# Linear attention in a one-core graph network: context taken from the normed rows, the last front's norm and softmaxes moved, attention of a joint over five PSUM banks

## The chip, the cores and the metric

One core of one Trainium2 chip runs the whole program in one launch. The metric is the device time in microseconds (us); the median of three runs stands for a kernel. A profile of one execution comes with it.

## The reference

`x` has 3125 rows of 256. After a layernorm the rows go two ways that are added at the end: a relational graph network of two passes over 53,125 edges (gather a row, multiply it with a relation's row, sum by target, three 256x256 products, tanh), and four transformer layers with linear attention:

```
h = layernorm(x) * g1 + b1                      # 3125 x 256, hence k, v: 3125 x 256
q = softmax over each head's 32 channels of (h @ Wq) * scale
k = softmax over the 3125 rows of (h @ Wk) * scale
v = h @ Wv
context = k^T v, per head (8 heads, 32 x 32)
x = x + (q @ context) @ Wo + bo
x = x + gelu(layernorm(x) * g2 + b2 @ W1 ...) @ W2 + b2      # 256 -> 1024 -> 256
```

A last stage (mixture of four experts and a shared network) follows. All is computed in float32.

## The kernel before

**Tiles.** The rows are 25 tiles of 125 (T), in 5 groups of 5 (GT, NG). A layer needs its whole context before any row can go on, so each layer is split: a *front* (norm, q, k, v, both softmaxes, the group's share of the context) runs for a group of rows of layer l+1 while the *feed* part (attention product, norm, up, gelu, down) of layer l works on the next group.

**Stages.** `iteration(lay, gi)` runs the feed of group gi and beside it, from gi = 1 on, the front of group gi-1 of the next layer (class `Front`). The last group's front has nothing beside it but graph work: `joint(la)` runs it (class `Alone`), closes the context, multiplies it by Wo (`cwo`), and does attention, norm and turning for the first group of the layer. For layer 0 all five fronts run as `Alone` before `joint(0)`. So there are 20 fronts: 5 alone in the prologue, 12 beside a feed, 3 alone in the joints of layers 1 to 3. Below, "joint 1" is the one of layer 1.

**A front.** VectorE (DVE) takes statistics (`norm_stats`, L422) and norms tile j into `xha` (L943, L1053; two buffers); TensorE (PE) turns it (L452); ScalarE (ACT) applies gain and shift into `hTa` (L1562, L1638); PE multiplies by Wk and Wv in one product of 512 columns (L1911, L2011) and by Wq in one of 256 (L1915, L2016), each over two chunks of 128 channels, and float32 takes two instructions for each; ACT copies k and v to `kv5` (L1574, L1651), q to `qrow` (L1582, L1658). DVE keeps the running maximum of k (L953), which is turned, reduced, spread again by PE (L1926) and subtracted (L971). ACT takes the exponentials (L1589, L1593), DVE normalizes q (L995 to L1001), PE forms the context, 2 x 5 products of 129 columns (128 of v and a column of ones; L1934), and turns q (`turn_q`), which ACT copies to `qT_all`. `add_context` (L978) adds the group's context, faded by the change of the maximum.

**Closing a joint** (L2073 on): context divided by its sums and masked to the heads on DVE (L1120, L1123), turned on PE (L2083), copied (L1130), times Wo plus bo (L2089, L2091), copied (L1133). `attend` (L1959) for 5 tiles alternates between two banks, so that tile pairs wait for `add_attention` (L1015).

**Graph work** is put between by hand: POOL gathers rows (L753, L760; two gathers per step of 128 edges in the first pass, one in the second) into a ring of 8 steps; DVE builds one-hot keys (L891) and multiplies (L900); PE sums 2 steps a unit into `ps_seg` (L1879), 257 columns each; DVE adds to `acc` (L880). `STEPS_JOINT` and `STEPS_GROUP` say how many steps each stage holds, `marks` and `joint_marks` where; `upto(k)` in each engine's program issues units up to a mark. Each engine works its own list strictly in order.

## Time and profile before

| | us |
|---|---|
| median of 3 runs | 2602.88 (2590.5 to 2606.51) |
| the profiled execution | 2572.66 |
| its span | 2570.9 |
| PE busy | 2110.7 (82%) |
| DVE busy | 1284.4 (50%) |
| ACT busy | 733.5 (29%) |
| POOL busy | 1362.8 (53%) |

"Busy" is the time in which an engine has an instruction in its datapath; the rest is waiting. The granted clock is the share of 2.4 GHz that TensorE was given: its two levels are 1.2 GHz (0.5) and 2.4 GHz (1.0). In a timeline a row merges instructions of one line; "x4" are four instructions, the number behind the start is their length, and the brackets say how long the engine had been idle before and what ended it. The length of the last matmul of a row is modelled, so prices of matmuls are read between starts.

### The profile page before, as it was taken

The numbers are of one execution on the slowest core, as the hardware profiler recorded it, in microseconds if no ns is written. First come the engines' busy times: TensorE is split into PE (matmuls) and PEld (weight loads), VectorE is DVE, ScalarE is ACT, GpSimd is POOL, SyncE is SP. The second block draws the span as 40 slices with busy tenths as digits, with TensorE's granted clock in tenths as the row PEclk, the third lists the DMA queues.
The fourth block names the chain that finished last, engine by engine and source line by source line (L and its number), as shares of the span: only waits on it lengthen the run. The fifth ranks groups of instructions, "written<-read, shape, count | busy, mean of one in ns | idle before, by whom it ended". The sixth has DMA issues, their size and how long they took to land.

```text
span 2570.9 us, 33841 instructions
## 1 busy us (share of the span) xinstructions
PE 2110.7 (82%) x11194; PEld 1738.3 (68%) x11194; DVE 1284.4 (50%) x3362; ACT 733.5 (29%) x1970; POOL 1362.8 (53%) x1377
## 2 busy tenths in 40 slices
PE   3776778987777789878778797998879888889998
PEld 1544667766656577666467686776657777778897
DVE  6765325435453254354523544746665555466533
ACT  3332123323221133232212332322222211223443
POOL 6566666656646666566466125657546665651000
PEclk9897889988888899889788899999989999999999
DMA  7466655545645555456455225545535555550000
GB/s 205 133 181 197 184 164 163 165 145 162 195 141 173 174 155 163 146 155 196 138 177 172 74 70 174 174 145 166 183 123 157 162 168 159 166 98 17 10 20 20
DMA packets 191190, 370.85 MB, mean 144 GB/s; under 512 B 36227, under 2 KB 122548, under 8 KB 191044
## 3 DMA queue, kind: packets, MB, share of 16 engines
q0 software_dynamic: 78272, 225.07, 30.8%
q1 hardware_dynamic: 92856, 128.48, 15.6%
q10 hardware_dynamic: 19916, 15.44, 2.0%
q8 instruction: 81, 1.33, 0.2%
q14 instruction: 65, 0.53, 0.1%
HBM read 304.76 MB, written 64.95 MB: 144 GB/s over the span
## 4 chain that ended last, share of the span: by engine, by line
PE 55%; DVE 14%; another core or an unknown queue 10%; issue 9%; POOL 3%; DMA 3%; ACT 2%; DVEq 1%; ACTq 0%; SPq 0%
PE ps_seg L1879 10%; PE ps_down L1984 8%; PE ps_hid L1975 7%; PE ps_kv L1911 4%; PE ps_x L1959 3%; DVE xg L900 3%; PE ps_down L2207 2%; POOL xg L753 2%; PE ps_kv L2207 2%; PE ps_x L452 2%; PE ps_hid L2227 2%; PE ps_hid L452 2%; DMA xg<-h_rows,idx_tab 2%; PE ps_x L1915 2%
## 5 line engine op out<-in xcount | busy, mean ns | idle before, releaser
L1879 PE MATMUL ps_seg<-xg,hot 128*125 128x257 f32 x1664 | 474.3, 416 | 207.9 <-DVE xg L900 159.7
L753 POOL DMA_INDIRECT xg<-xn_rows,idx_tab x416 | 416.8, 1002 | 419.1 <-PE ps_seg L1879 250.3
L753 POOL DMA_INDIRECT xg<-h_rows,idx_tab x416 | 426.2, 1025 | 284.2 <-PE ps_seg L1879 152.7
L1879 PEld LDWEIGHTS ps_seg<-xg,hot 128*125 128x125 f32 x1664 | 310.9, 202 | 293.4 <-DVE xg L900 152.1
L760 POOL DMA_INDIRECT rg<-relation_rows,idx_tab x416 | 422.4, 1016 | 128.0 <-issue 128.0
L1975 PE MATMUL ps_hid<-hT,wff 128*128 128x125 f32 x3200 | 414.1, 284 | 27.0 <-issue 22.3
L1975 PEld LDWEIGHTS ps_hid<-hT,wff 128*128 128x128 f32 x3200 | 407.6, 201 | 40.7 <-issue 28.2
L1624 ACT ACTIVATE gT<-ps_hid,b1p 128x125 f32<-128x125 f32 x800 | 225.4, 369 | 677.7 <-remote 322.3
L1984 PE MATMUL ps_down<-wff,gT 128*125 128x256 f32 x1600 | 374.8, 386 | 11.1 <-issue 10.7
L900 DVE TENSOR_TENSOR xg<-xg,rg 128x512 f32<-128x512 f32 x416 | 286.0, 687 | 129.8 <-DMA xg<-h_rows,idx_tab 67.7
L1984 PEld LDWEIGHTS ps_down<-wff,gT 128*125 128x125 f32 x1600 | 301.0, 192 | 56.1 <-issue 12.8
L1039 DVE TENSOR_TENSOR xres<-xres,ps_down 125x256 f32<-125x256 f32 x100 | 40.3, 419 | 333.9 <-remote 160.3
L891 DVE TENSOR_TENSOR hot<-iota_t,key_tab 128x250 f32<-128x250 f32 x416 | 170.9, 411 | 7.8 <-issue 5.3
L1015 DVE TENSOR_TENSOR xres<-xres,ps_x 125x256 f32<-125x256 f32 x100 | 38.8, 418 | 184.7 <-PE ps_x L1959 133.1
L1539 ACT ACTIVATE kv<-ps_kv 125x512 f32<-125x512 f32 x74 | 44.2, 597 | 288.4 <-PE ps_kv L1911 198.0
L1959 PE MATMUL ps_x<-cwo,qT_all 128*125 128x256 f32 x400 | 109.3, 417 | 9.4 <-DVE xres L1015 6.9
L880 DVE SCALAR_TENSOR_TENSOR acc<-ps_seg,in_tile,acc 125x257 f32 x208 | 100.4, 483 | 32.7 <-PE ps_seg L1879 14.3
L1911 PE MATMUL ps_kv<-wqkv,hTa 128*125 128x512 f32 x240 | 114.7, 601 | 0.0
L1614 ACT ACTIVATE hT<-ps_x,ln2p 128x250 f32<-128x250 f32 (+1 forms) x120 | 56.6, 523 | 192.2 <-PE ps_x L452 176.8
L1959 PEld LDWEIGHTS ps_x<-cwo,qT_all 128*125 128x125 f32 x400 | 83.1, 211 | 30.1 <-DVE xres L1015 9.7
L424 DVE BATCH_NORM_STATS2 stat<-xres 125x6 f32<-125x256 f32 x200 | 70.1, 413 | 0.0
L1911 PEld LDWEIGHTS ps_kv<-wqkv,hTa 128*125 128x125 f32 x240 | 46.4, 193 | 34.1 <-issue 30.1
(285 smaller groups left out, 2702.0 us busy)
## 6 DMA issues: line engine op xcount, KB each, us to landing
second_relation_rows<-rg SPq DMA_DIRECT2D x104, 512.0 KB
rg<-second_relation_rows SPq DMA_DIRECT2D x104, 512.0 KB
wff<-L_mix_W ACTq DMA_DIRECT2D x8, 1024.0 KB
xg<-xn_rows,idx_tab POOLq DMA_INDIRECT x416
rg<-relation_rows,idx_tab POOLq DMA_INDIRECT x416
xg<-h_rows,idx_tab POOLq DMA_INDIRECT x416
h_rows<-rg SPq DMA_DIRECT2D x25, 112.0 KB
xres<-x POOLq DMA_DIRECT2D x5, 560.0 KB, 8.7
```

Source lines behind the costliest of these rows:

```text
L452: ins = pe.transpose(dst[:, c * T:(c + 1) * T], rows[:, c * P:(c + 1) * P], ident[0:T, 0:T])
L753: pool.indirect_dma_start(xg[:, k, 0:D], None, rows, bass.IndirectOffsetOnAxis(ap=idx_tab[:, step, 0:1], axis=0))\
L760: pool.indirect_dma_start(rg[:, k, :], None, rel_d, bass.IndirectOffsetOnAxis(ap=idx_tab[:, step, 1:2], axis=0))\
L891: dve.tensor_tensor(hot[:, s:s + UNIT, :], iota_t[:, :].unsqueeze(1).broadcast_to([EP, UNIT, T]), key_tab[:, at:at + UNIT].unsqueeze(2).br ...
L900: dve.tensor_tensor(m, m, r, ALU.mult).then_inc(s_msg, 1)
L1624: ins = act.activation(gT[:, j % 2, ff, :], ps_hid[hf][:, f * T:(f + 1) * T], ACT.Gelu, bias=b1p[:, ff:ff + 1])
L1879: ins = pe.matmul(ps_seg[u // UW % 2][0:T, 0:AW], hot[:, s % RING, :], xg[:, s % RING, :], start=s % WIN == 0, stop=s % WIN == WIN - 1)
L1911: ins = pe.matmul(ps_kv[0:T, :], hTa[:, j % 2, c, :], wqkv[:, c, D:], start=c == 0, stop=c == KC - 1)
L1959: ins = pe.matmul(ps_b[j % 2][0:T, :], q[:, c * T:(c + 1) * T], cwo[:, c, :], start=c == 0, stop=c == KC - 1)
L1975: ins = pe.matmul(ps_hid[hf][:, f * T:(f + 1) * T], w1[:, c, ff * P:(ff + 1) * P], hT[:, j, c, :], start=c == 0, stop=c == KC - 1)
L1984: ins = pe.matmul(ps_down[j % 2][0:T, :], gT[:, j % 2, f, :], w2[:, f, :], start=f == 0, stop=f == FC - 1)
L2207: ins = pe.matmul(ps_two[j % 2][0:T, 0:D], gT[:, j % 2, m * KC + c, :], wg[g][:, m, c, :], start=m == 0 and c == 0, stop=m == 2 and c == K ...
```

## The change

1. **No v product.** The context of a head is (k^T xhat) Wv, with xhat the normed row before gain and shift. `xha` and v are gone; the normed rows go to `x5`, which shares a buffer with k (`kx5`, 256 + 257 columns). A tile has one product of 512 columns, for q and k; ACT copies 256 columns of k and 256 of q out of the same bank. The context products have 257 columns in place of 129, into two banks (`ps_beside`: `ps_kv`, `ps_hid[1]`; `ps_alone`), and `add_context` adds 2 x 257 columns.
2. **Closing.** `close_context` divides each half as it comes; four transposes (128 x 128); gain and shift applied on DVE; four products of 128 columns with Wv; mask; Wo into `ps_dn`, with bo multiplied ahead.
3. **The last front's norm** (new class `Last`): statistics of its rows beside the last tiles of the last FFN group, its norm right behind `add_ffn(4)`. The q softmax of the front before it (sum, scale, turn) goes behind that, into the joint.
4. **Softmaxes of the last front in two parts** (tiles 0 to 2, tiles 3 and 4), in joints 0 to 3.
5. **Attention in a joint over five banks** (`ps_att`), with no wait for `add_attention`.
6. Waits: norm(0) of a front waits for the context before it; up(0), second half, waits for `add_context` (layers 0 to 2, gi > 1); the wait for the next layer's q, k, v weights goes from group 0 to group 1; Wv and ln1 are loaded after the Wv product. Numbers of graph steps stay.

```diff
 def norm(self, j):                               # Front, DVE
-    dve.wait_ge(s_tra, self.tn + (j + 1 if j else 2))
-    dve.tensor_scalar(xha[:, j % 2, :], self.row(j), mv[:, j, 0:1], rstd[:, j:j + 1], ALU.subtract, ALU.mult)\
+    if j == 0:
+        dve.wait_ge(s_ctx, self.grp + 1 - self.back)
+    dve.tensor_scalar(self.x5[:, j, 0:D], self.row(j), mv[:, j, 0:1], rstd[:, j:j + 1], ALU.subtract, ALU.mult)\
         .then_inc(s_xha, 1)
...
 def joint(la, upto, one):                        # DVE
     m = joint_marks(la)
-    f = Alone(la, NG - 1) if la else fronts[-1]
+    f = lasts[la]
     if la:
-        f.head(lambda: one(m["head"]))
+        upto(0)
+        before_last[la].q_sum()
+        before_last[la].q_scale()
+        f.k_max(1)
         upto(m["head"])
-        front_tiles(f, None, None, [m[f"tile{j}"] for j in range(GT)], upto, one)
+        f.k_max(2)
+        f.q_max(0)
+        f.q_shift(0)
+        upto(m["tile2"])
+        f.k_max(3)
+        f.q_sum(0)
+        f.q_scale(0)
+        upto(m["tile4"])
     front_end(f, m, upto)
...
 def front_end(f, m, upto):                       # DVE
+    upto(m["spread"])
     f.k_max(GT - 1)
     f.k_top()
-    f.q_max()
-    upto(m["spread"])
-    f.k_shift()
-    f.q_shift()
-    f.q_sum()
-    f.q_scale()
+    f.q_max(1)
+    f.k_shift(0)
+    f.k_shift(1)
+    f.q_shift(1)
+    f.q_sum(1)
+    f.q_scale(1)
     upto(m["ctx"])
-    f.add_context()
+    f.close_context()
...
+def close_context(self):                         # Last, DVE
+    dve.wait_ge(s_kf, self.grp + 1)
+    dve.wait_ge(s_cacc, self.grp + 1)
+    cm = self.cm
+    for c in range(KC):
+        if c == 0:
+            dve.wait_ge(s_c0, self.la + 1)
+        else:
+            dve.wait_ge(s_ctx, self.grp + 2)
+        cm(dve.scalar_tensor_tensor(ctxacc[:, c, :], ctxacc[:, c, :], kfade[:, c:c + 1],
+                                    self.ps_ctx[c][:, 0:AW], ALU.mult, ALU.add))
+        cm.wait()
+        cm(dve.reciprocal(rsum[:, c:c + 1], ctxacc[:, c, D:AW]))
+        cm.wait()
+        cm(dve.tensor_scalar(ctxacc[:, c, 0:D], ctxacc[:, c, 0:D], rsum[:, c:c + 1], None, ALU.mult))
+    cm.wait()
+    dve.sem_inc(s_cacc, 1)
...
 def iteration(lay, gi, upto, one, early):        # DVE
+    a = lasts[lay + 1] if lay < L - 1 and is_last(gi) else None
...
+    if a:
+        for j in range(3):
+            a.stat(j)
...
     b.add_ffn(3)
     b.add_ffn(4)
+    if a:
+        a.stat(3)
+        a.stat(4)
+        norm_rest(dve, a.ln)
+        a.norm(0)
+        a.norm(1)
+        f.add_context()
+        for j in range(2, GT):
+            a.norm(j)
+        before_last[lay + 1] = f
+        return
...
 def qkv(self, j):                                # Front, PE
     pe.wait_ge(s_kve, self.tn + (j + 1))
-    for c in range(KC):
-        ins = pe.matmul(ps_kv[0:T, :], hTa[:, j % 2, c, :], wqkv[:, c, D:], start=c == 0, stop=c == KC - 1)
-    ins.then_inc(s_kv, 1)
     pe.wait_ge(s_qe, self.tn + (j + 1))
     for c in range(KC):
-        ins = pe.matmul(ps_q[0:T, :], hTa[:, j % 2, c, :], wqkv[:, c, 0:D], start=c == 0, stop=c == KC - 1)
+        ins = pe.matmul(ps_kv[0:T, :], hTa[:, j % 2, c, :], wqkv[:, c, 0:2 * D], start=c == 0, stop=c == KC - 1)
     ins.then_inc(s_q, 1)
...
     if la:                                       # joint, PE
-        upto(m["head"])
         f.turn(0)
-        front_tiles(f, None, None, [m[f"tile{j}"] for j in range(GT)], upto)
+        f.turn(1)
+        f.qkv(0)
+        f.turn(2)
+        f.qkv(1)
+        upto(0)
+        f.turn(3)
+        f.qkv(2)
+        for j in range(GT):
+            before.turn_q(j)
+        upto(m["head"])
+        f.turn(4)
+        f.qkv(3)
+        upto(m["tile2"])
+        f.qkv(4)
+        upto(m["tile4"])
     front_end(f, m, upto)
...
+        ins = pe.matmul(ps_kv[:, c * P:(c + 1) * P], wqkv[:, f, 2 * D + c * P:2 * D + (c + 1) * P],
+                        cwo[:, f, c * P:(c + 1) * P], start=f == 0, stop=f == KC - 1)
...
     for j in range(GT):
-        b.attend(j)
+        b.attend_alone(j)
...
 def front_end(f):                                # ACT
-    f.k_exp()
-    f.q_exp()
-    for j in range(0, GT, 2):
-        f.qT_out(j)
+    f.k_fade()
+    f.qT_out(0)
+    f.k_exp(0)
+    f.k_exp(1)
+    f.q_exp(1)
+    f.qT_out(2)
+    f.qT_out(4)
```

In `front_end` on PE the turns of q stand around the context now: turn_q(0), turn_q(1), k_spread, graph unit, turn_q(2), context, turn_q(3), turn_q(4).

## Rows read from the trace of the kernel before

**Rows 1.** The page's busy shares and granted clock in 40 slices

```profile
PE 2110.7 (82%) x11194; PEld 1738.3 (68%) x11194; DVE 1284.4 (50%) x3362; ACT 733.5 (29%) x1970; POOL 1362.8 (53%) x1377
...
PEclk9897889988888899889788899999989999999999
```

**Rows 2.** Busy time by stage: joint 0's fronts, a group, joints 1 and 3

```profile
core 0: us, PE busy (x) PEld busy (x) DVE busy (x) ACT busy (x) POOL busy (x), PEclk, DMA share, GB/s
108.00:202.00 94.00, 77.91 (x328) 52.81 (x328) 63.85 (x148) 36.25 (x77) 64.95 (x64) 0.91 0.57 169
428.00:520.00 92.00, 77.86 (x416) 65.51 (x415) 45.57 (x122) 29.60 (x76) 56.11 (x56) 0.91 0.54 162
686.00:766.00 80.00, 51.96 (x198) 35.70 (x198) 46.33 (x119) 17.39 (x35) 36.56 (x36) 0.77 0.52 158
...
1841.00:1917.00 76.00, 55.23 (x219) 38.46 (x218) 50.64 (x129) 17.50 (x35) 27.97 (x27) 0.82 0.41 128
```

**Rows 3.** PE's timeline at full clock: start, length, instructions

```profile
192.00 1.88 PE L2011 MATMUL ps_kv<-wqkv,hTa 128*125 128x512 f32 x4
193.72 1.03 PE L2016 MATMUL ps_x<-wqkv,hTa 128*125 128x256 f32 x4
194.58 2.40 PE L1934 MATMUL ps_hid<-wff 125*128 125x129 f32 x20
196.81 0.59 PE L452 MATMUL ps_hid<-ident,xh 125*128 125x125 f32 x4
197.24 1.03 PE L1879 MATMUL ps_seg<-xg,hot 128*125 128x257 f32 x4
198.11 1.88 PE L2011 MATMUL ps_down<-wqkv,hTa 128*125 128x512 f32 x4
```

**Rows 4.** What PE waited for in the group from 428 to 520

```profile
PE ps_seg L1879 <- DVE xg L900: 7.8, 1, 7.8
PE ps_x L452 <- DVE qrow L1001: 4.1, 1, 4.1
```

**Rows 5.** PE's timeline, joint 1, and the first product of joint 3

```profile
706.42 3.62 PE L2011 MATMUL ps_kv<-wqkv,hTa 128*125 128x512 f32 x4
...
724.96 0.38 PE L452 MATMUL ps_hid<-ident,kmax 125*128 125x125 f32 x2
...
742.03 0.38 PE L2083 MATMUL ps_kv<-ident,kdiag 128*128 128x128 f32 x2
...
745.78 1.96 PE L1959 MATMUL ps_x<-cwo,qT_all 128*125 128x256 f32 x8
...
1855.79 3.03 PE L2011 MATMUL ps_kv<-wqkv,hTa 128*125 128x512 f32 x4
```

**Rows 6.** DVE's timeline, joint 1, and the last FFN sum before joint 3

```profile
686.45 0.75 DVE L1039 TENSOR_TENSOR xres<-xres,ps_down 125x256 f32<-125x256 f32 x2 [2.08 <-PE ps_down L1984]
687.34 1.49 DVE L995 TENSOR_REDUCE qm<-qrow 125x40 f32<-125x1280 f32 x1
...
689.30 1.49 DVE L1001 TENSOR_TENSOR qrow<-qrow,qm 125x1280 f32<-125x1280 f32 x1
696.79 0.61 DVE L978 SCALAR_TENSOR_TENSOR ctxacc<-ctxacc,kfade,ps_kv 128x129 f32<-128x129 f32 x2 [6.00 <-remote]
...
703.84 0.83 DVE L1055 TENSOR_SCALAR xha<-xres,mv,rstd 125x256 f32<-125x256 f32 x2
...
753.25 0.75 DVE L424 BATCH_NORM_STATS2 stat<-xres 125x6 f32<-125x256 f32 x2
...
1841.01 0.75 DVE L1039 TENSOR_TENSOR xres<-xres,ps_down 125x256 f32<-125x256 f32 x2
```

**Rows 7.** ACT's timeline, joint 1: one tile, and k's exponential

```profile
714.37 0.38 ACT L1539 ACTIVATE qrow<-ps_x 125x256 f32<-125x256 f32 x1 [0.27 <-PE ps_x L2016]
715.46 0.80 ACT L1642 ACTIVATE hTa<-ps_x,ln1p 128x125 f32<-128x125 f32 x2 [0.70 <-PE ps_x L452]
717.18 0.60 ACT L1539 ACTIVATE kv<-ps_kv 125x512 f32<-125x512 f32 x1 [0.91 <-PE ps_kv L2011]
...
731.54 1.27 ACT L1589 ACTIVATE kv<-kv 125x1280 f32<-125x1280 f32 x1 [4.74 <-DVE kv L971]
```

**Rows 8.** POOL's timeline in a group: gathers of the first pass

```profile
455.35 0.94 POOL L753 DMA_INDIRECT xg<-xn_rows,idx_tab  x1 [0.30 <-issue]
456.60 0.95 POOL L760 DMA_INDIRECT rg<-relation_rows,idx_tab  x1 [0.30 <-issue]
457.85 0.95 POOL L753 DMA_INDIRECT xg<-xn_rows,idx_tab  x1 [0.30 <-issue]
```

**Rows 9.** What DVE's idle time ahead of L978 ended on, all 20 contexts

```profile
L978 DVE SCALAR_TENSOR_TENSOR ctxacc<-ctxacc,kfade,ps_kv x24: 341/344/351, 426.3 to 1847.5; 128x129 f32<-128x129 f32 x24
...
  remote: 31.4, 8
```

More of the change, by code:

```diff
@@ L425, in norm_stats, with norm_rest @@
             between()
+            norm_rest(dve, chain, between)
+        def norm_rest(dve, chain, between=lambda: None):
             hold(dve, chain.s, chain.base + chain.n)
@@ L453, in transpose_rows, with parts_done, part_of @@
             return ins
+        PARTS = (slice(0, 3), slice(3, GT))
+        def parts_done(grp, part=0):
+            return grp + grp // NG + (part + 1)
+        def part_of(j):
+            return int(j >= PARTS[1].start)
         def pair(j):
@@ L1361, in z_beside @@
                                               ALU.mult).then_inc(s_exh, 1)
-            fronts = [Alone(0, ga) for ga in range(NG)]
+            lasts, before_last = [Last(la) for la in range(L)], {}
+            fronts = [Alone(0, ga) for ga in range(NG - 1)] + [lasts[0]]
             dve.wait_ge(s_const, 1)
@@ L1806, in _ @@
             act.wait_ge(s_wqkv, 5 * 16)
-            fronts = [Alone(0, ga) for ga in range(NG)]
+            fronts = [Alone(0, ga) for ga in range(NG - 1)] + [Last(0)]
             fronts[0].norm_out(0)
@@ L1961, in attend, with attend_alone @@
                     ins.then_inc(s_ao, 1)
+                def attend_alone(self, j):
+                    if j == 0:
+                        pe.wait_ge(s_cwr, self.lay + 1)
+                        pe.wait_ge(s_hT, self.tn + 1)
+                    q = at_tile(qT_all, self.gi * GT + j)
+                    for c in range(KC):
+                        ins = pe.matmul(ps_att[j][0:T, 0:D], q[:, c * T:(c + 1) * T], cwo[:, c, :], start=c == 0, stop=c == KC - 1)
+                    ins.then_inc(s_ao, 1)
                 def turn(self, j):
@@ L2267, in mu_beside @@
                         ins.then_inc(s_elg, 1)
-            fronts = [Alone(0, ga) for ga in range(NG)]
+            fronts = [Alone(0, ga) for ga in range(NG - 1)] + [Last(0)]
             pe.wait_ge(s_const, 1)
```

355 lines of the change are left out of this document (232 added, 123 removed).

## The prediction

> **What bounds the kernel now.** I read the busy shares first: PE is at 82%, and in every slice the other engines are lower [rows 1]. So a microsecond of PE's own stream counts wherever PE is the one that others wait for. The table by stage says where that is: in a group of 92 us PE is busy 77.9 us, in joint 1 only 52.0 of 80 us, at a granted clock of 0.77 in place of 0.91 [rows 2]. There are thus two limits: in the groups the number of columns that PE streams, in the joints a chain from engine to engine. POOL is third: its gathers start every 1.25 us [rows 8], two per step in the first pass, 2.5 us a step. A group of 26 to 28 steps needs 65 to 70 us of its 92, a joint of 18 steps 45 of 80, but beside the prologue's fronts POOL issued 64 gathers, 80 of 94 us at this pace [rows 2]: there the gathers nearly bind.
>
> **Prices.** Between starts at full clock, four instructions of 512 columns take 1.72 us, four of 256 take 0.86, twenty of 129 take 2.23, four of 257 take 0.87 [rows 3]. So one instruction costs 0.43, 0.216, 0.112 and 0.217 us: time goes with the columns down to 129.
>
> **1. Products of the front.** A tile has eight instructions now, 1.72 + 0.86 = 2.58 us; afterwards four of 512 columns, 1.72. It saves 0.86 us, 4.3 us a front. The context grows from 20 x 0.112 = 2.2 to 20 x 0.217 = 4.3 us, 2.1 us a front. Net 2.2 us of stream for each of 20 fronts, 44 us in all; four closings give back some 1 us each (four more instructions' worth of transposes and eight of 128 columns, at 0.112).
> The Trainium skill ("TensorE: Matmul & The Clock Gate", "Back-to-back issue gap") gives a sustained spacing of 81 ns at 128 columns and 131 ns at 512, both set by weight load and product together. By that rule the 256 columns taken away would be worth about half as much and the wider context nearly nothing; an estimate from its figures is 1.6 us a front. Here the spacing grows 3.8 times from 129 to 512 columns, so the trace disagrees, and I go by the rows.
>
> **2. Groups (12 with a front beside).** In nine of them (gi 1 to 3) the wider context stands where PE waits anyway: behind down(4), DVE needs add_ffn 0.75, sum 1.49, reciprocal 0.4, scale 1.49 = 4.1 to 4.4 us [rows 6] until q can be turned, while PE has a unit, a turn and the context, 3.3 us, then 5.4. In the group at 428 PE waited 4.1 us for that scale [rows 4]. So of the 2.1 us about 1 us is felt and a group saves 3.3 us; bounds 2.2 (nothing hidden) and 4.3 (all hidden). In the three last groups (gi 4) the context belongs to the joint as I cut it, so they save 4.3. Sum 30 + 13 = 43 us at full clock, 47 at the group's 0.91. I take 40, since a part of what PE saves will meet waits such as the 7.8 us for DVE's product [rows 4]; bounds 27 (12 x 2.2) and 52.
> The new wait before up(0)'s second half names add_context (two adds of 257 columns, an estimated 1.0 us from the 0.61 for both halves at 129 [rows 6]); behind it PE has all of the group queued, and ACT's gelu waits for that. DVE reaches add_context before that half up is due, one half up of 1.8 us later: cost 0, bound 2 us a group. The single bank for q and k makes PE wait for two ACT copies of 0.38 in place of one of 0.60 and one of 0.38 [rows 7]; several microseconds of up and down stand between two tiles' products, so 0; in the joint two banks alternate. Without this cover it would be 0.2 to 0.8 us a tile.
> The five extra statistics in the last groups and norm_rest run on DVE (half idle, [rows 1]); the first three come before k_shift, 1.2 us, within its idle time; the weights' later wait and the later issue of Wv and ln1 (ACT's queue, about 2 us of issuing in a stretch where ACT idles; the turned rows behind them are due 10 us later) cost 0, bound 2 us a joint.
>
> **3. Prologue.** Five fronts save 2.2 us each, 11 us, but POOL runs nearly without a pause there. I take 2 us, bounds 0 and 10.
>
> **4. Joints 1 to 3, up to the first product.** Now the way is add_ffn (686.45), q's sum and scale, add_context at 696.8, five statistics, aggregation and the root (to 703.84), norm, turn, gain: first product at 706.42, 20 us; in joint 3, from 1841.01 to 1855.79, 14.8 us [rows 5, 6]. Of joint 1's 20 us, 6.0 are a hold: DVE and PE's followers waited for "remote" although the context's instructions had been recorded before it. Afterwards q's sum and scale (3.4 us) are behind, three statistics are done early and the rest with the root run beside the context (4.3 us plus a unit). Norm(0) waits for the context, since both use one buffer: about 5.3 us after down(4), then norm 0.4, turn 0.2, gain 0.8 [rows 7]: first product near 7 us. Saving 7.8 in joint 3; in joints 1 and 2 between 6 (the hold stays) and 13. I take 8.
>
> **5. From the first product to the turn of k's maximum.** Now 706.42 to 724.96, 18.5 us [rows 5]. PE saves 4.3 us in products but takes over the five turns of the front before (1.1 us), and DVE has sum and scale of that front, half a q softmax and four graph units in a row with the maxima: my list of DVE comes out at 17.6 us. Saving 1, bounds -3 and 4.
>
> **6. From there to the attention.** Now 20.8 us to 745.78 [rows 5]. Full-width q and k operations of 1.49 us each [rows 6] go in parts: 0.9 and 0.6 (by elements), with the first parts of q taken before. k shifted in two parts, exponentials behind them (0.8 and 0.5 by elements, from 1.27 [rows 7]), context from 4 us after the turn's start to 8.5 (full clock) or 12.5; closing halves 1.15 us each, the first beside the second half's products; closing to the attention 4.5 us against 3.8 now, from 742.03 [rows 5]. That gives 15.8 us. Saving 5, bounds 1 and 7.
>
> **7. Attention and statistics.** Now the last statistic starts at 753.25, 7.5 us after 745.78 [rows 5, 6], since PE waits for banks. 20 instructions at 0.216 are 4.3 us, the last add and statistic follow: saving 2.9; at the lower clock of 1.2 GHz the stream is 8.6 us and nothing is saved.
>
> Sum of 4 to 7: 16.9 us a joint at full clock. But the joint's clock is 0.77 [rows 2], and PE's parts, 4.3 us of context among them, then take twice as long; I cut it to 12 us. Three joints: 36, bounds 18 and 60. Joint 0 has only 6 and 7 and gets 6, bounds 0 and 9.
>
> **Sum.** 40 + 2 + 36 + 6 = 84 us; all low ends 45, all high ends 131. The profiled execution took 2572.66 us for a span of 2570.9, and the median of the runs shown is 2602.88, 30 us above it, with 16 us from lowest to highest: the profiled one is no slower than the others. From its own time the sum gives 2489; I subtract from the median: **2519 us**, -3.2%. The likeliest case's own range is 2490 to 2550. Faster or slower here means by over 1% (26 us), about what a measurement of this kernel can tell from no change.
>
> **Rivals.**
> *A. Only the columns count* (15%). The joints stay bound by DVE's order: graph units stand ahead of the maxima now, and DVE is at 46 of 80 us in a joint [rows 2]. Then 27 + 2 and about 4 us a joint, 12: 40 us, 2563. For it: step 5 leaves little; against: step 4's moved 3.4 us and root are plainly off the way.
> *B. Gathers become the bound* (8%). 2.5 us a step [rows 8] is 385 us for the 154 steps of a layer in the first pass; a group needs 70 of 92 us, so after a saving of 4 there is room, but a ring of eight steps bridges 20 us only. If joints 1 and 2 and their next groups give half back, the loss is some 30 us of the 84: 2550. It would show as DVE idle on the gather of rg.
> *C. More than summed* (15%). Fewer instructions (some 800 of PE's 22,388, both kinds), less idle, so less time at 1.2 GHz; holds gone. High ends: 2480 or so.
> *D. The wider contexts are held longer* (4%), the one that ends on the other side. Before eight of the 20 add_contexts DVE waited 31.4 us in all for "remote" [rows 9], time after the context's recorded instructions. The context is twice as long now, and norm(0), the add and the next group's up wait for it. If each of the 20 were held 6 us more, 120 us would be lost against 84 won: 2639. It decides from 4.2 us a context on; now the mean is 1.6. Against: the stream rate falls there, in joint 3 nothing was held.
> My forecast itself gets 58%.
>
> The range that leaves out no more than 2 in 10: 2480 (C's side) to 2562 (A just outside or at the edge). Faster by over 1% (under 2577): the forecast, C, B and nearly all of A: 0.91; within 1%: 0.05; slower: 0.04.
>
> **What would show it.** In the new profile the products of 512 columns number 4 a tile with none of 256 behind them, and a context spans 4.3 us at full clock (step 1). Groups with a front take about 88 us (2). From the last FFN sum to the first product 7 us, or 14 with a hold (4); to the turn of the maximum 17 to 18 (5); to attention 16 (6); attention with no gap, under 5.5 us (7); a joint near 67 us from 80. Prologue unchanged within a few us (3). The forecast is wrong if groups keep their 92 us (then PE's stream wasn't the bound), if a joint's DVE waits move ahead of k_max(4), or if the time ahead of the adds grows past 4 us each.

## The result, and the profile after

| | time, us (median; lowest to highest; runs) | ratio to before, 95% interval |
|---|---|---|
| before, same chip | 2595.76 (2582.38 to 2609.82; 20) | |
| changed | 2585.02 (2571.23 to 2605.03; 20) | 0.9957 (0.9937 to 0.9976) |
| forecast | 2519 (2480 to 2562) | 0.968 |

The change gives 11 us where 84 were forecast. The profiled execution of the changed kernel took 2595.55 us (span 2593.7), 10 us over its own median, where the one of before took 2572.66, some 23 us under its median. Between these two profiles the stages are therefore read with some 34 us of slack (they say +23 us where the medians say -11).

The page of the changed kernel: PE's busy time [rows 1], its clock, the chain that ended last, and the groups of GELU and of the FFN sum.

```profile
PE 2079.1 (80%) x10834; PEld 1697.8 (65%) x10834; DVE 1297.2 (50%) x3398; ACT 701.9 (27%) x1978; POOL 1353.0 (52%) x1377
...
PEclk9877889889978888899778998999989999999999
...
PE 50%; another core or an unknown queue 14%; DVE 13%; issue 9%; POOL 7%; DMA 3%; ACT 2%; DVEq 1%; SPq 0%; ACTq 0%
...
L1742 ACT ACTIVATE gT<-ps_hid,b1p 128x125 f32<-128x125 f32 x800 | 225.2, 369 | 668.4 <-remote 336.6
...
L1059 DVE TENSOR_TENSOR xres<-xres,ps_down 125x256 f32<-125x256 f32 x100 | 40.3, 419 | 352.4 <-remote 227.5
```

The same three kinds of line on the page of before, which stood there and which the prediction did not use:

```profile
PE 55%; DVE 14%; another core or an unknown queue 10%; issue 9%; POOL 3%; DMA 3%; ACT 2%; DVEq 1%; ACTq 0%; SPq 0%
...
L1624 ACT ACTIVATE gT<-ps_hid,b1p 128x125 f32<-128x125 f32 x800 | 225.4, 369 | 677.7 <-remote 322.3
...
L1039 DVE TENSOR_TENSOR xres<-xres,ps_down 125x256 f32<-125x256 f32 x100 | 40.3, 419 | 333.9 <-remote 160.3
```

PE has 31.6 us less to do, and PE's share of the chain falls by five points. But "another core or an unknown queue" and POOL rise by four points each, about 100 us apiece. On one core there is no other core: this is time for which the trace has no releaser.

Busy time by stage of the changed kernel (as [rows 2]): joint 0's fronts, a window about the group gi 2 of layer 0 (its up products start at 439.0, those of the next group at 536.6), joints 1 and 3.

```profile
112.00:208.00 96.00, 65.41 (x244) 42.26 (x242) 61.56 (x139) 30.21 (x69) 69.28 (x66) 0.86 0.58 176
436.40:534.00 97.60, 75.46 (x392) 62.64 (x392) 44.41 (x118) 27.56 (x74) 57.26 (x57) 0.90 0.51 151
708.70:784.70 76.00, 47.25 (x162) 31.82 (x162) 47.38 (x125) 15.52 (x37) 31.70 (x33) 0.75 0.47 147
1866.50:1934.50 68.00, 53.97 (x203) 38.59 (x202) 51.80 (x135) 15.63 (x37) 27.76 (x27) 0.83 0.44 139
```

Joint 3 takes 68.0 us in place of 75.1, 7 of the 12 us that the forecast took off a joint, but joint 1 still takes 76.0 (79.1 before), and a group that should have come down to 88 takes 97.6. What happens in that group (POOL, then DVE, then PE):

```profile
443.76 1.33 POOL L767 DMA_INDIRECT xg<-xn_rows,idx_tab  x1 [6.68 <-PE ps_seg L2049]
...
462.99 0.95 POOL L774 DMA_INDIRECT rg<-relation_rows,idx_tab  x1 [0.30 <-issue]
...
466.88 0.42 DVE L1059 TENSOR_TENSOR xres<-xres,ps_down 125x256 f32<-125x256 f32 x1 [18.22 <-remote]
...
451.50 3.62 PE L2164 MATMUL ps_down<-wff,gT 128*125 128x256 f32 x16
468.65 2.05 PE L2049 MATMUL ps_seg<-xg,hot 128*125 128x257 f32 x4 [13.53 <-DVE xg L914]
```

POOL issues 16 gathers without a pause, 443.8 to 463.9. Down(0) is recorded at 451.5 to 455.1, yet the sum that waits for it alone starts at 466.9, 3 us after the last gather. PE's records run ahead of what the other engines see, here by 11.8 us. I call such a stretch a hold. Joint 1 shows the same between the last graph product and add_context (DVE first, then POOL):

```profile
743.30 0.68 DVE L914 TENSOR_TENSOR xg<-xg,rg 128x512 f32<-128x512 f32 x1
754.83 0.48 DVE L1141 SCALAR_TENSOR_TENSOR ctxacc<-ctxacc,kfade,ps_x 128x257 f32<-128x257 f32 x1 [10.85 <-remote]
...
726.17 1.17 POOL L767 DMA_INDIRECT xg<-xn_rows,idx_tab  x1 [12.84 <-PE ps_seg L2049]
...
750.44 0.95 POOL L774 DMA_INDIRECT rg<-relation_rows,idx_tab  x1 [0.31 <-issue]
```

So theory H: TensorE is held while POOL's gathers come in long bursts. Rival J: the gathers are innocent, and the gain is missing for reasons of the change's own order.

### The profile page after: what moved, and what is told of

Read it like the earlier page. It is cut to its first block, busy times and chain, and to the rows that moved or that the text cites. A ratio compares the mean times of both kernels' runs of the same rounds, so it can differ in the third digit from the quotient of the medians.

```text
span 2593.7 us, 33141 instructions
## 1 busy us (share of the span) xinstructions
PE 2079.1 (80%) x10834; PEld 1697.8 (65%) x10834; DVE 1297.2 (50%) x3398; ACT 701.9 (27%) x1978; POOL 1353.0 (52%) x1377
## 4 chain that ended last, share of the span: by engine, by line
PE 50%; another core or an unknown queue 14%; DVE 13%; issue 9%; POOL 7%; DMA 3%; ACT 2%; DVEq 1%; SPq 0%; ACTq 0%
PE ps_seg L2049 10%; PE ps_hid L2155 7%; PE ps_down L2164 7%; POOL xg L767 5%; PE ps_kv L2082 4%; DVE xg L914 3%; PE ps_x L2127 3%; POOL rg L774 3%; PE ps_down L2437 2%; PE ps_kv L2437 2%; PE ps_x L459 2%; PE ps_hid L2457 2%; PE ps_hid L459 2%; DMA xg<-h_rows,idx_tab 2%
## 5 line engine op out<-in xcount | busy, mean ns | idle before, releaser
L2049 PE MATMUL ps_seg<-xg,hot 128*125 128x257 f32 x1664 | 480.9, 420 | 251.0 <-DVE xg L914 170.1
L774 POOL DMA_INDIRECT rg<-relation_rows,idx_tab x416 | 416.8, 1002 | 128.5 <-issue 128.5
L1059 DVE TENSOR_TENSOR xres<-xres,ps_down 125x256 f32<-125x256 f32 x100 | 40.3, 419 | 352.4 <-remote 227.5
L2082 PE MATMUL ps_kv<-wqkv,hTa 128*125 128x512 f32 x240 | 122.4, 635 | 13.8 <-ACT hTa L1687 13.8
L1660 ACT ACTIVATE kx<-ps_kv 125x256 f32<-125x256 f32 x74 | 28.5, 385 | 352.5 <-PE ps_kv L2082 199.1
L1031 DVE TENSOR_TENSOR xres<-xres,ps_x 125x256 f32<-125x256 f32 x80 | 30.8, 418 | 171.9 <-PE ps_x L2127 121.5
L1732 ACT ACTIVATE hT<-ps_x,ln2p 128x250 f32<-128x250 f32 (+1 forms) x120 | 56.6, 524 | 209.8 <-PE ps_x L459 172.0
L2127 PE MATMUL ps_x<-cwo,qT_all 128*125 128x256 f32 x320 | 89.7, 426 | 0.0
L2082 PEld LDWEIGHTS ps_kv<-wqkv,hTa 128*125 128x125 f32 x240 | 48.4, 203 | 51.8 <-issue 32.3
L2127 PEld LDWEIGHTS ps_x<-cwo,qT_all 128*125 128x125 f32 x320 | 69.3, 217 | 14.0 <-issue 0.2
```

What stands on the lines that cost most here:

```text
L774: pool.indirect_dma_start(rg[:, k, :], None, rel_d, bass.IndirectOffsetOnAxis(ap=idx_tab[:, step, 1:2], axis=0))\
L2049: ins = pe.matmul(ps_seg[u // UW % 2][0:T, 0:AW], hot[:, s % RING, :], xg[:, s % RING, :], start=s % WIN == 0, stop=s % WIN == WIN - 1)
L2082: ins = pe.matmul(ps_kv[0:T, :], hTa[:, j % 2, c, :], wqkv[:, c, 0:2 * D], start=c == 0, stop=c == KC - 1)
L2127: ins = pe.matmul(ps_b[j % 2][0:T, :], q[:, c * T:(c + 1) * T], cwo[:, c, :], start=c == 0, stop=c == KC - 1)
```

## The experiments

The expectations speak of a "fast machine" or "machine of 2377 us" and a "slow machine" or "machine of 2585 us". The runs fell on six chips, of two kinds. On chips 0, 2, 5, 6 and 12 the kernel before took 2374 to 2379 us; on chip 14 2581 and 2585, like the 2596 of the result. I call them free and held chips. Three names that the expectations use: theory M, the hold comes with the chip; theory B, on a held chip the gathers' completions pile up and TensorE hardly runs while there is a backlog; rival D of the bench, each gather costs TensorE a fixed time whatever the spacing (not the prediction's rival D).

**1 and 2. The relation gathers left out, before and after.** Free chip 2. Of the two gathers of a step one goes, and with it its wait for the store of the old rows; the waits of DVE and SP are lowered to match, and the relation rows are set to zero (all this left out below):

```diff
-                    if g == 0:
...
-                        pool.indirect_dma_start(
-                            rg[:, k, :], None, rel_d, bass.IndirectOffsetOnAxis(ap=idx_tab[:, step, 1:2], axis=0))\
-                            .then_inc(s_edge[k // UNIT], 16)
```

> The kernel before with the relation gathers of the first pass left out (POOL issues one gather a step where it issued two; the relation rows are zeros, so the edge term of the first pass is missing; everything else stands). Theory H, held: the changed kernel got its gain in the stream and lost it again because TensorE is held back while POOL's first-pass gathers run in long bursts (a burst of 12 gathers at 432.7 to 447.7 us of before, with VectorE waiting 13.24 us until 450.09). Without every second gather the bursts are half as long, and this kernel is faster than before by 40 to 100 us: 2500 to 2555 us, ratio 0.96 to 0.985. Rival J, joints only: the gathers beside the groups are hidden and what is missing is missing from the joints; ratio 0.99 to 1.0 here.

> The changed kernel with the same edit as the run before it (relation gathers of the first pass left out, relation rows zero). Theory H: with the bursts halved the change's own gain shows, and this kernel is faster than the one of before with the same edit by 45 to 84 us, ratio between the two 0.965 to 0.983; against before 0.93 to 0.965. Rival J: the change is worth as little without the gathers as with them, ratio between the two 0.993 to 0.999.

Measured: 2296.27 us, ratio 0.9668 (0.9648 to 0.9688), and 2217.27 us, ratio 0.9337 (0.9317 to 0.9356). The two are 79 us apart, a ratio of 0.966: the change is worth what was summed. But the kernel before took 2377 us on this chip, so the chip could be the reason as well as the gathers. A repeat on free chip 6 gave 2296.12 and 2223.34 us, 73 apart. On a held chip this pair was never measured.

**3. TensorE alone beside gathers.** Plain products that wait for nothing; VectorE marks every eighth (CHUNK is 8).

```diff
+for k in range(CHUNK):
+    ins = pe.matmul(bank[ph % 2][0:T, 0:cols], w[:, 0:T], mv[:, 0:cols], start=True, stop=True)
+ins.then_inc(s_pe, 1)
...
+pool.indirect_dma_start(xg[:, n % RING, :], None, io["x"],
+                        bass.IndirectOffsetOnAxis(ap=idx[:, k:k + 1], axis=0)).then_inc(s_g[n % RING], 16)
```

> A bench of its own, none of the reference's work: TensorE runs plain float32 products in six phases of 240 (120 of the wide): 125 columns alone; 125 with 48 gathers of 125 rows on POOL beside them; 257 columns alone; 257 with 48 gathers; 125 beside twelve plain loads of 1 MB on SP's queue; 125 alone. VectorE writes a mark after every eighth product. Theory H: the marks come later in the phases with gathers, eight products take 1.3 to 4 times as long as alone, and the phase ends 1 to 3 us after the last gather or later. Rival: the marks are as close with gathers as without (within 3%), and what held TensorE in the kernel is something else (a semaphore, a missing operand).

Measured on chip 2: 1.75 us for eight products of 125 columns with and without gathers, 3.47 us for 257 columns. Theory H fell, on that chip.

**4 to 6. The whole kernels on one free chip.** Chip 0, both as they are.

> The changed kernel as it is, once more. In the first experiments' call the kernel before took 2377 us, where it had taken 2596 us beside the changed kernel. Theory M, the machine: what swallowed the gain (TensorE held back beside the gathers) differs from chip to chip, and on a chip on which the kernel before takes about 2377 us the change shows most of what was summed: ratio 0.965 to 0.98. Theory H, held by the gathers alone: 0.993 to 0.998 wherever it runs. If this call falls on a chip on which the kernel before takes about 2596 us, both theories say 0.994 to 0.998.

> The kernel before as it is, for a profile from the same chip as the other runs of this call. Theory M: where its time is near 2377 us its profile shows waits for 'remote' on VectorE and ScalarE well under the 160 and 322 us of the earlier profile, and groups of the first pass 10 to 20 us shorter. Theory H: the holds are as many, and the difference of 8% lies elsewhere (clock).

Measured: the changed kernel 2310.87 us against 2378.97, ratio **0.9712** (0.9693 to 0.9731), a gain of 68 us; the profiled kernel before 2373.82 us. The chain of the kernel before on this chip, and after it that of the changed one:

```profile
PE 59%; DVE 14%; POOL 11%; issue 7%; DMA 4%; ACT 1%; DVEq 1%; ACTq 0%; SPq 0%
```

```profile
PE 62%; DVE 11%; POOL 10%; issue 6%; DMA 6%; ACT 1%; DVEq 1%; ACTq 0%; SPq 0%
```

The unknown queue is gone, and so is every wait for "remote". So theory M stands, as far as one held and five free chips can tell: the change is worth 68 us on a free chip, 11 on the held ones.

Beside it, columns alone: the second contraction half of the k,v product left out, so k and v are made of half the features.

```diff
-                    for c in range(KC):
-                        ins = pe.matmul(ps_kv[0:T, :], hTa[:, j % 2, c, :], wqkv[:, c, D:], start=c == 0, stop=c == KC - 1)
+                    for c in range(1):
+                        ins = pe.matmul(ps_kv[0:T, :], hTa[:, j % 2, c, :], wqkv[:, c, D:], start=True, stop=True)
```

> The kernel before with the second of the two contraction halves of the k,v product left out (k and v are made of half the features; 2 x 2 instructions of 512 columns a tile go, no other engine's work changes). TensorE's stream is shorter by 4 x 0.215 = 0.86 us a tile, 100 tiles, 86 us in all. If TensorE's columns set the groups (steps 1 and 2 of the prediction): 50 to 86 us less, ratio 0.965 to 0.98. If the groups are set by something else (gathers, VectorE, waits): 0 to 20 us, ratio above 0.992.

Measured: 2317.70 us, ratio 0.9742 (0.9717 to 0.9767): 61 us of the 86. The 12 groups with a front fell from 1102.2 to 1049.2 us, 53.0 us, where their 60 tiles lost 51.6 us of stream. TensorE's columns do set the groups, microsecond for microsecond where the gathers do not hold them. The prologue, whose 25 tiles lost 21.5 us, did not move (223.1 and 223.2 us), and joints 1 to 3 gave 3.6 of 12.9 us.

**7 and 8. Chip 14, a held one: the bench again, and the attention over two banks.**

> The bench of products beside gathers once more (none of the reference's work). On the first machine 8 products of 125 columns took 1.75 us with and without gathers beside them. If this call falls on a machine where the kernel before takes about 2596 us: theory M (TensorE itself is held there while POOL's gathers run) has 8 products at 2 to 7 us in the phases with gathers, and 1.75 us alone; the rival (the held time comes from the kernel's own waits) has 1.75 us in all phases. On a machine of 2377 us both say 1.75 us everywhere.

The bench took 438.28 us in place of 357.81. VectorE's marks on chip 14, one per eight products; the gathers run from 70.3 to 130.1:

```profile
73.30 0.06 DVE L97 MEMSET mark<- 128x1 f32 x1 [1.69 <-issue]
75.26 0.06 DVE L97 MEMSET mark<- 128x1 f32 x1 [1.90 <-PE ps L84]
80.30 0.06 DVE L97 MEMSET mark<- 128x1 f32 x1 [4.98 <-remote]
91.61 0.06 DVE L97 MEMSET mark<- 128x1 f32 x1 [11.25 <-remote]
128.04 0.06 DVE L97 MEMSET mark<- 128x1 f32 x1 [36.37 <-issue]
137.91 0.22 DVE L97 MEMSET mark<- 128x1 f32 x2 [9.81 <-remote]
```

The windows of the same bench on chip 14: alone, beside 48 gathers, behind them, beside plain loads. Then the window with the gathers on chip 2. Columns as in [rows 2], without ACT.

```profile
13.80:69.30 55.50, 55.25 (x480) 55.09 (x480) 1.77 (x30) 0.00 (x0) 1.00 0.00 1
69.40:130.30 60.90, 21.57 (x128) 18.23 (x128) 0.37 (x8) 45.53 (x48) 0.62 0.35 102
130.30:178.00 47.70, 43.22 (x352) 41.72 (x352) 1.36 (x23) 0.00 (x0) 0.87 0.01 4
...
329.20:382.00 52.80, 52.66 (x480) 52.47 (x480) 1.73 (x30) 0.00 (x0) 1.00 0.58 240
```

```profile
69.30:130.30 61.00, 52.66 (x480) 52.47 (x480) 1.80 (x32) 45.52 (x48) 0.96 0.35 102
```

An engine that waits for nothing did 128 of its 480 instructions (two to a product) in 61 us, 93 of them in the first 10.4; plain loads at 240 GB/s cost it nothing. POOL and the DMA queues do exactly the same on both chips: 48 gathers, 102 GB/s. This is the hold, shown without any of the kernel's own waits. By the marks it begins after the first 4 or so gathers (the mark at 75.26 is the last on time), and it ends 7.8 us after the last of 48. From this I worked out the backlog of theory B: 48 gathers worked off in 137.9 - 70.3 = 67.6 us, 1.41 us each, against 1.25 us at which POOL issues. In the kernel 16 gathers in a row would end (1.41 - 1.25) x 16 = 2.6 us late; above, the late sum came 2.9 us after the burst. That is an estimate that fits, not a proof of a backlog.

The Trainium skill ("SBUF — State Buffer", "Who interferes with whom") says, of contention for the memory's ports, that PE and ACT never wait on anyone. On free chip 2 the bench agrees for PE (1.75 us with and without gathers). On chip 14 PE did wait: 128 instructions in place of 480; whether ports have a part in that no run here shows.

> The changed kernel with one part undone: the joints' attention goes over two banks again, as in the kernel before (the product of tile 2 waits for the sum of tile 0 or 1, and so on). Step 7 of the prediction put the five banks at 2.9 us a joint, four joints, 11.6 us at full clock and nothing at the lower one. So on a chip where the kernel before takes about 2377 us: 6 to 12 us slower than the changed kernel there (2311 us), ratio to before 0.973 to 0.977. Rival: the statistics on VectorE set the end either way; within 2 us of the changed kernel, ratio 0.971.

```diff
-                    b.attend_alone(j)
+                    b.attend(j)
```

On DVE `add_attention_alone` becomes `add_attention` with it.

Measured on chip 14: 2569.08 us, ratio 0.9949 (0.9915 to 0.9982), no different from the changed kernel's 0.9957. The five banks cannot be seen in the time of a held chip, though the attention's 20 instructions start over 6.65 us in place of 4.10. This run's profile is worth more than its edit: it is a second profile of the changed kernel on a held chip, at its own median (2569.6 us). Its 12 groups with a front take 1204.2 us and its joints 1 to 3 222.2, against 1202.3 and 233.6 in the profile of before.

**9. How close may gathers stand?** Chip 14.

> A bench of its own, none of the reference's work: nine phases of 320 float32 products of 125 columns that wait for nothing, 70 us each when alone; beside them nothing; 32 gathers of 128 rows with no pause (1.25 us apart); with a memset of 64, 256, 512 and 1024 columns behind each gather; 32 gathers of 64 rows; 32 plain transfers of the same 128 rows of 1 KB on SP's queue; nothing. On the machine where the kernel before takes about 2590 us, theory B (a backlog: a gather's completion is worked off there every 1.4 us, from the earlier bench's 67.6 us for 48 gathers, and TensorE hardly runs while there is a backlog) has the phase without a pause at 100 to 115 us, and phases with a spacing over 1.5 us (memset of 256 columns and more) at 70 to 75 us. Rival D (each gather costs TensorE a fixed time, whatever the spacing): 100 to 115 us in all phases with gathers. Plain transfers: 70 us if POOL's own way of issuing matters, 100 if any transfer of many rows does. On a machine of 2377 us: 70 us in all phases.

The seven windows of the bench with traffic beside TensorE: no pause, memset of 64, 256, 512, 1024 columns behind each gather, gathers of 64 rows, plain transfers. The first six are about as long as their traffic lasts; the plain transfers were all issued in the first 19.4 us of the last, some 0.6 us apart.

```profile
86.60:126.60 40.00, 18.86 (x122) 16.36 (x122) 0.36 (x7) 29.57 (x31) 0.69 0.34 99
190.90:235.40 44.50, 35.76 (x199) 31.13 (x199) 0.65 (x11) 35.70 (x64) 0.69 0.32 92
287.70:337.00 49.30, 49.19 (x450) 49.19 (x451) 1.65 (x28) 40.06 (x63) 1.00 0.28 82
358.40:416.00 57.60, 57.50 (x526) 57.50 (x527) 1.93 (x33) 46.89 (x63) 1.00 0.25 72
429.10:498.00 68.90, 68.82 (x630) 68.82 (x631) 2.33 (x40) 59.69 (x63) 1.00 0.21 60
500.70:539.00 38.30, 15.25 (x99) 13.44 (x100) 0.29 (x5) 28.02 (x31) 0.68 0.18 52
608.40:678.00 69.60, 69.52 (x636) 69.52 (x637) 2.33 (x40) 0.00 (x0) 1.00 0.21 62
```

By the gathers' start times the spacings are 1.26, 1.39, 1.55, 1.81, 2.19 and 1.21 us, and the 320 products last 103.9, 96.4, 70.3, 70.3, 70.3 and 107.3 us. The point lies between 1.39 and 1.55 us, where 1.41 was expected. Above it a gather costs TensorE nothing, so the bench's rival D is out. Half the rows help nothing, and as many rows of the same size, moved by SP with plain transfers (last window), cost nothing.

**10 to 13. The kernels paced.** A pause behind every gather of the first pass (behind the second of a step stand the same two lines, with `2 * step + 2`), nothing left out; chip 14 for the first.

```diff
+                        pool.memset(pad[:, 0:PACE], 0.0).then_inc(s_pad, 1)
+                        pool.wait_ge(s_pad, 2 * step + 1)
```

> The changed kernel with the same pause behind each gather of the first pass (nothing left out). Theory B: on the machine of 2590 us it is faster than the kernel before by 2 to 7%, and as both paced kernels are bound by the gathers in part, it is ahead of the paced kernel before by 20 to 60 us. On the machine of 2377 us it is slower than the changed kernel there (2311 us) by 60 to 200 us. Rival D: slower than before on both machines.

Measured with 256 columns: 2515.71 us, ratio **0.9738** (0.9688 to 0.9789), where the changed kernel has 0.9957. Its gathers and chain:

```profile
704.66 0.95 POOL L770 DMA_INDIRECT xg<-xn_rows,idx_tab  x1 [0.27 <-POOL pad L782]
705.62 0.33 POOL L774 MEMSET pad<- 128x256 f32 x1
706.22 0.95 POOL L779 DMA_INDIRECT rg<-relation_rows,idx_tab  x1 [0.27 <-PE ps_seg L2056]
```

```profile
PE 37%; POOL 35%; issue 12%; DVE 9%; DMA 5%; ACT 0%; another core or an unknown queue 0%; DVEq 0%; POOLq 0%; SPq 0%; ACTq 0%
```

At 1.55 us a gather the unknown queue falls from 14% of the chain to nothing, and POOL takes its place: the gathers themselves are now the bound. Off the chain some waits for "remote" are left, most of them ACT's ahead of GELU:

```profile
ACT gT L1749 <- remote: 86.9, 12, 9.6
```

Not one of them stands in the first pass. The first is at 1530 us, behind the start of the second pass at 1500, whose gathers have no pause and for the most part start 1.25 us apart. So within one run the holds are gone where the gathers are spaced and there where they are not. Joint 1 takes 67.5 us (76.0), joint 2 70.1 (75.1), joint 3 64.9 (68.0).

The paced kernel before and shorter pauses fell on free chip 12:

> The kernel before with a memset of 192 columns and a wait for it behind each gather of the first pass (nothing left out): the spacing is put at 1.5 us, from 1.39 with 64 columns and 1.55 with 256 in the bench. Theory B (backlog, worked off every 1.4 us): on the machine of 2585 us the holds go here too, 2520 to 2560 us, ratio 0.975 to 0.99; its groups were less bound by the gathers than those of the changed kernel. Rival: only the changed kernel gains from the pauses, ratio 0.995 to 1.01. On the machine of 2377 us: 2390 to 2450 us.

> The changed kernel with the same pause (192 columns, nothing left out). Theory B: on the machine of 2585 us 2460 to 2505 us, ratio 0.953 to 0.97, and 40 to 70 us ahead of the paced kernel before: then what the change is worth was there all along and the holds took it. Rival: the change is worth as little with pauses as without, within 20 us of the paced kernel before. On the machine of 2377 us: 2320 to 2400 us.

> The changed kernel with a shorter pause (96 columns, nothing left out): the spacing is put at 1.42 us, at the 1.39 to 1.41 where the bench's holds end. Theory B: on the machine of 2585 us 2440 to 2500 us where the spacing lies just above the point, as slow as 2540 where it lies below; on the machine of 2377 us 2315 to 2360 us. Rival D (each gather costs TensorE a fixed time): no better than the longer pause's loss, 2540 to 2600 us.

Measured: 2491.42 us, ratio 1.0475 (1.0442 to 1.0508); 2457.74 us, 1.0332 (1.0300 to 1.0364); 2412.26 us, 1.0136 (1.0105 to 1.0168), and once more on free chip 6 1.0142. All three were slower than their expectations for a free chip. Where nothing is held a pause only costs, 101 us at 1.41 us of spacing and 147 at 1.50 against the changed kernel's 2311 us. Between the two kernels with 192 columns the change is worth 34 us of its 68: nearly none of it in the groups (1151.9 to 1148.3 us over twelve), since gathers bind there, and 26 in the joints (223.1 to 196.7). The kernel before with pauses was never measured on the held chip.

**14 and 15. Two steps where nothing is held and the gathers are thin.** Free chip 5, relation gathers left out: first the changed kernel, with the attention over two banks as well; then the kernel before, with the second half of k and v's product left out as well.

> The changed kernel with the relation gathers of the first pass left out and the joints' attention over two banks again. Without the second edit it took 2217 and 2223 us on the fast machine. Step 7 of the prediction (2.9 us a joint, four joints): 2229 to 2235 us there, 9 to 12 us more. Rival (the statistics set the end either way): 2218 to 2224 us. On the slow machine theory B (only dense gathers make it slow) has this kernel at 2230 to 2320 us, ratio 0.86 to 0.90; rival S (slower whatever runs) at 2420 us or more.

> The kernel before with the relation gathers of the first pass left out, and the second contraction half of the k,v product left out too (TensorE's stream 86 us shorter). Beside the relation gathers that half was worth 61 us of the 86; without them the kernel before took 2296 us. If the missing 25 us were lost to the gathers: 2210 to 2222 us here (74 to 86 us less). Rival (they were lost to VectorE and the joints' chains): 2230 to 2245 us, as without the edit 61 less. On the slow machine theory B: 2210 to 2310 us; rival S: 2400 us or more.

Measured: 2234.54 us, ratio 0.9377 (0.9351 to 0.9404), and 2230.73 us, ratio 0.9367 (0.9339 to 0.9396). The first is 11 to 17 us over the same kernel with five banks (4 to 10 by the ratios, since chips differ by some us, and there the intervals overlap), and its attention starts over 6.72 us in place of 4.17: the trace shows step 7's term, the time only just. The second is 66 us (71 by the ratios) under its partner, between the 61 and the 86 expected and at the edge of the rival's range: some of what TensorE saves is lost whatever the gathers do. Without them the prologue gives 7.5 of its 21.5 us, where it gave nothing, the groups 45.7 of 51.6, the joints 7.3 of 12.9. How much of the rest VectorE takes stays open.

## Why the prediction was wrong, step by step

The stages of four pairs, from the starts of the first up product of each group and the last FFN sum of each layer in the profiled executions (us; the last column is the forecast):

| stage | after - before, held (result) | changed and paced - before, held | free chip 0 | free chip 2, thin gathers | forecast |
|---|---|---|---|---|---|
| prologue with joint 0 | +6.2 | +1.3 | +1.8 | -7.9 | -8 |
| 3 first groups | 0.0 | +1.4 | +1.3 | +0.9 | 0 |
| 12 groups with a front | +26.4 | -33.4 | -37.8 | -36.3 | -40 |
| joints 1 to 3 | -14.5 | -31.1 | -28.2 | -36.5 | -36 |
| last layer and end | +4.6 | +3.7 | +6.4 | -3.1 | 0 |
| span | +22.8 | -58.1 | -56.6 | -83.0 | -84 |

The two profiles of free chip 0 lie some 12 us closer together than the medians (68 us). With nothing held and thin gathers each term comes within 4 us of the forecast, and the whole within 1. Some of that is luck. The forecast was made for the kernel with all its gathers. The same pair on chip 6 has -7.2, -1.3, -31.0, -38.2 and -2.0 us. And the 36 us of the joints come out for another reason than the one given: steps 4 and 6 saved 6.2 and 2.3 us a joint on the mean of chip 2, where 8 and 5 were foreseen, while the cut from 16.9 to 12 us was made for the clock.

The +26.4 us of the groups in the first column is mostly slack: the profile of the changed kernel with two banks (7 and 8 above) has the groups at +1.9 and the joints at -11.4. So on a held chip the groups gave about nothing by the profiles, and what shows of the change shows in the joints. The profile of before lies 23 us under its median, so even if all of that stood in the groups, they gave no more than 21 of the 40 us.

The steps, where nothing is held, in joint 1 of the changed kernel on chip 0 (PE, then the last FFN sum of DVE):

```profile
593.54 2.33 PE L2102 MATMUL ps_kv<-kx 125*128 125x257 f32 x10
595.71 2.33 PE L2102 MATMUL ps_hid<-kx 125*128 125x257 f32 x10
...
600.28 1.90 PE L2192 MATMUL ps_kv<-wqkv,hTa 128*125 128x512 f32 x4
...
618.13 0.68 PE L459 MATMUL ps_hid<-ident,kmax 125*128 125x125 f32 x2 [1.69 <-DVE kmax L969]
...
636.66 1.96 PE L2137 MATMUL ps_x<-cwo,qT_all 128*125 128x256 f32 x8
...
592.87 0.75 DVE L1059 TENSOR_TENSOR xres<-xres,ps_down 125x256 f32<-125x256 f32 x2 [2.09 <-PE ps_down L2164]
```

- **Step 1** held: the context's two halves start 2.17 us apart, 4.3 us for both, and a tile has four instructions of 512 columns [rows 3].
- **Step 2** (40 us, its waits at nothing): 38 and 36 us where nothing is held, 33 in the paced kernel. On the held chips the term was not there: +26.4 us in the result's profile, +1.9 in the second one.
- **Step 3 and joint 0** (8 us): 7.9 us with thin gathers, nothing with all of them, as its caution "POOL runs nearly without a pause" said. Of rival B's "some 30 us of the 84" the two free columns show 26 (83.0 against 56.6): 9.7 us in the prologue, 8.3 in the joints, 9.5 in the last layer and end. Its sign, DVE idle on the gather of rg, did not come: 128.4 us against 128.0 before. So a loss of B's size comes with the gathers; by what way it comes is not shown.
- **Step 4** (first product near 7 us after the last FFN sum [rows 5, 6]): 7.1 us above, and 7.0, 7.0 and 7.9 us in the result's own profile. Right even on the held chip; joint 1 came down from 19.6 us there, from 13.9 on free chip 0, where no hold was left to remove.
- **Step 5** (17.6 us to the turn of k's maximum): 17.9 above, 19.9, 18.7 and 19.4 in the result's profile.
- **Step 6** (15.8 us to the attention): 18.5 above, against 20.5 before on the same chip, so 2 us and not 5 (joint 2 0.5, joint 3 0.9 the other way): the step's own miss where nothing is held. In the result's profile joints 1 and 2 took 32.0 and 32.3 us, joint 3 21.3. Here the joints lost, in the hold of 10.85 us shown above. Paced, joint 1 is back at 18.5, but step 5 takes 23.8 there: DVE waits up to 5.1 us for a relation gather.
- **Step 7** (20 instructions in 4.3 us): 4.2 us against 6.7; the saving is 2.55 us a joint, 2.9 foreseen.
- **Two readings** were off without weight: in the first slice of [rows 1] DVE and POOL (6 and 6) are above PE (3), not lower, and PE's instructions of both kinds fell by 720, not by some 800.

**The step that failed** is in steps 2 and 6: the 40 us of the groups and the 5 us a joint rest on "a microsecond of PE's own stream counts wherever PE is the one that others wait for" and on an undisturbed chain, and so on a PE that is free to run its stream. On the held chips the groups gave +1.9 and +26.4 us in place of -40, and step 6 took 32.0 and 32.3 us in joints 1 and 2 in place of 15.8. The hold was left out of the sum: the prediction did see holds and priced them, in rival D and in [rows 9], but only ahead of add_context: 31.4 us. The answer to [rows 9] in the changed kernel is 30.2 us (8.5 at L994 and 21.7 at L1141), so in total the contexts were not held longer, and D as it was priced is not what happened. But 21.7 of the 30.2 us now stand ahead of the closing contexts of joints 1 and 2, 10.9 us in each, where the kernel before waited for nothing; there D's mechanism acted, and it is most of what step 6 lost:

```profile
L994 DVE SCALAR_TENSOR_TENSOR ctxacc<-ctxacc,kfade,ps_hid x16: 472/476/478, 105.3 to 1873.4; 128x257 f32<-128x257 f32 x16
...
  remote: 8.5, 3
```

```profile
L1141 DVE SCALAR_TENSOR_TENSOR ctxacc<-ctxacc,kfade,ps_x x4: 475/480/483, 229.0 to 1904.4; 128x257 f32<-128x257 f32 x4
...
  remote: 21.7, 3
```

The same word stood on the page of before with 322.3 us beside GELU and 160.3 beside the FFN sum, and with a tenth of the chain: a hold of the whole engine, met by whichever consumer came next. As I read it, it was a bound of its own, and on the chip where the time was to be forecast it belonged into the sum as a resource that the change does not touch.

**What is shown and what is not.** Shown: TensorE, waiting for nothing, is held on chip 14 beside gathers 1.26 and 1.39 us apart and not at 1.55, and is not held on chip 2 at 1.25; on free chip 0 the change is worth 68 us; on chip 14 pauses remove the unknown queue from the chain, bring step 6 back to 18.5 us and make the changed kernel 66 us faster than the kernel before there, where the result has 11. Argued only: that the hold alone took the change's gain. The bursts are as long in both kernels (with starts less than 1.5 us apart counted as one burst, the time of gathers beyond the first 5 us of each adds to 428 us before and 440 after), so why a shorter stream did not shorten what lies between them stays open. In the changed kernel the FFN sums wait longer for "remote" (227.5 against 160.3 us) and POOL's share of the chain is larger, so more of the way runs through held stretches; that is a description, not a cause. How much of the paced kernel's gain is the pause's own, apart from the change, is open too: the kernel before with the same pause on a held chip would tell, and the pair with thin gathers there.

No version was best on both kinds of chip: the changed kernel as it is on free ones (0.971), the paced one on the held one (0.974).

## What to carry to other kernels

Read the word "remote" or "an unknown queue" on a one-core page as time of some engine that the trace cannot place: add it up over all consumers, look at what ran while it lasted, and treat it as a bound before pricing a shorter stream. A bench in which the suspected engine waits for nothing, with the suspected traffic beside it, told in one run what no reading of the kernel's trace could. Where nothing stands in the way, a sum of instruction durations by stage was good to some 10 us a stage here. A microsecond of the leading engine's stream was worth 0.7 to 0.8 us over the whole kernel (61 and 66 to 71 of 86), but that is a mean of unlike stages: 0.9 to 1.0 in the groups, where TensorE leads, and nothing in the prologue as long as the gathers bind there.

## What the runs showed of the hardware

- Chips of one type differ by 9% on one kernel (2374 to 2379 us on five, 2581 and 2585 on chip 14), and in the bench POOL and the queues did the same work on both kinds. With pauses step 6 of joint 1 takes 18.5 us on chip 14, as on chip 0 without them.
- On chip 14 gathers issued by POOL at 1.39 us of spacing or less hold TensorE: 122 instructions in 40 us where 450 went in 49 us at 1.55 us of spacing. It begins after some 5 us and ends 3 us after a burst of 16 and 8 us after one of 48. Gathers of 64 rows are no better than those of 128, and plain transfers of as many rows do nothing, though they are issued twice as densely. The granted clock was 0.69 on the mean of the held window and 1.00 in the one at 1.55 us.
- The held traces lack records. Semaphore events in the trace of before: 17,014 on the chip of the first profile, 33,674 on chip 0; in the bench 936 on chip 14 and 2,222 on chip 2. The missing ones are for the most part those of the gathers: 6,729 of 19,968 landings are in the trace of before, 19,953 in that of chip 0. All traces of chip 14 lack them, but not only where TensorE is held: in the bench window at 1.55 us, without a hold, 161 of 512 landings are there, and the first pass of the paced kernel lacks 22% of its landings and has no wait for "remote". So lost records mark that chip, and not the hold. The Trainium skill ("NOTIFIC — the notification-queue block", "7.1 Overflow: three behaviours, one of which stalls the engine") describes a block that, when its queues are full, drops records or stalls the producer. Lost records and a held engine are both seen here; whether they are that block's, and so whether the hold would vanish without a profile, no run here shows.
